# A bias matmul of 64 rows instead of 128, and the gate product issued behind the down product

## The reference

```python
# layer 0: a gated recurrence over the 64 steps, then a mixture of experts (8 experts, the best 2 per token)
gate = sigmoid(h @ Wh.T + z_t @ Wz.T + b);  h = tanh(h * (1 - alpha) + gate * z_t)
gh = einsum('nh,erh->ner', x, W_A)            # routing scores are the norms of gh over r (64)
y  = einsum('nef,ehf->neh', silu(gh @ W_B) * (x @ W_up), W_down)    # F = 512
x  = x + sum over the two chosen experts of y * weight
# layer 1: a tanh recurrence, then a feed-forward block with quantised weights and activations
h  = tanh(x_t @ Wx + b + h @ Wh)
x  = x + bitlinear(gelu(bitlinear(h, w1)), w2)
```

## Time and profile before

| | |
|---|---|
| median of 3 runs | 391.12 us (390.4 to 392.09) |
| the profiled execution's own time | 392.09 us |
| its span, first to last instruction | 390.1 us |
| mean granted TensorE clock | 0.952 of full speed |
| busy share of the span, TensorE | 84% |
| busy share of the span, VectorE | 70% |
| busy share of the span, ScalarE | 60% |
| busy share of the span, GpSimd | 55% |

### The profile page before, as it was taken

One profiled execution on the slowest core, in us unless ns is written; L12 is line 12 of the kernel. 1 busy time (PEld: TensorE's weight loads), 2 busy tenths in 40 slices (PEclk: granted clock), 3 DMA queues, 4 the chain that ended last, 5 costly groups with the idle time before them and its releaser, 6 DMA issues.

```text
span 390.1 us, 11984 instructions
## 1 busy us (share of the span) xinstructions
PE 327.8 (84%) x3816; PEld 231.3 (59%) x3817; DVE 272.2 (70%) x922; ACT 232.7 (60%) x733; POOL 214.0 (55%) x203
## 2 busy tenths in 40 slices
PE   2687777777577789999999999999987999999962
PEld 1444444444353357767777777777675777877841
DVE  5545555567996279587597878544456999999870
ACT  2356656565446446565656565565545878777871
POOL 5659999999804354454444745653115555562220
PEclk9999999998965699999999999999996999999998
DMA  8992185461592133222323332334213122221001
GB/s 209 201 396 103 42 297 188 160 244 64 193 337 75 29 124 89 66 86 68 90 64 91 90 89 73 96 82 79 69 39 97 32 83 69 81 67 41 29 29 40
DMA packets 22536, 42.95 MB, mean 110 GB/s; under 512 B 3986, under 2 KB 14610, under 8 KB 21604
## 3 DMA queue, kind: packets, MB, share of 16 engines
q0 software_dynamic: 6560, 23.17, 19.7%
q1 hardware_dynamic: 15664, 19.31, 15.7%
q10 hardware_dynamic: 276, 0.01, 0.0%
HBM read 28.97 MB, written 13.50 MB: 109 GB/s over the span
## 4 chain that ended last, share of the span: by engine, by line
PE 46%; DVE 14%; ACT 5%; issue 3%; DMA 2%; POOLq 0%; DVEq 0%; POOL 0%; ACTq 0%
PE bank L996 13%; PE bank L972 13%; PE bank L959 4%; PE bank L984 4%; DVE peak L1638 2%; PE bank L950 2%; DVE wrec L1599 2%; DVE h_lo L1669 1%; PE bank L952 1%; PE bank L1094 1%; PE bank L788 1%; PE bank L795 1%; DVE z_lo L1659 1%; PE bank L1111 1%; ACT z_hi L706 1%
## 5 line engine op out<-in xcount | busy, mean ns | idle before, releaser
L497 POOL DMA_INDIRECT xs<-hs_rows,row_of_slot x39 | 37.0, 948 | 72.3 <-PE bank L952 55.7
L788 PE MATMUL bank<-h_hi,wrec_hi 128*128 128x32 f16 x512 | 43.7, 181 | 29.3 <-ACT h_hi L595 27.8
L788 PEld LDWEIGHTS bank<-h_hi,wrec_hi 128*128 128x128 f16 x512 | 34.3, 97 | 56.0 <-ACT h_hi L595 49.6
L972 PE MATMUL bank<-wup_s,xt 128*128 x234 | 64.4, 385 | 0.0
L996 PE MATMUL bank<-wdn_s,wrec 128*128 x468 | 57.8, 273 | 0.3 <-ACT wrec L641 0.3
L996 PEld LDWEIGHTS bank<-wdn_s,wrec 128*128 128x128 f16 x468 | 45.2, 98 | 14.6 <-issue 1.1
L1492 DVE TENSOR_TENSOR wrec<-bank,wrec 128x512 f16<-128x512 f32 x39 | 27.0, 691 | 35.2 <-ACT wrec L641 34.8
L519 POOL DMA_INDIRECT z_lo<-y_rows,slot_i x32 | 31.1, 970 | 27.5 <-issue 26.4
L500 POOL DMA_INDIRECT gs<-gate_rows,row_of_slot x39 | 37.4, 958 | 11.9 <-issue 11.6
L1231 DVE TENSOR_TENSOR_SCAN bank<-bank,terms 128x128 f32<-128x128 f32 x64 | 27.6, 431 | 22.5 <-ACT bank L591 20.6
L788 PE MATMUL bank<-h_hi,wrec_lo 128*128 128x32 f16 x512 | 42.2, 178 | 0.0
(11 more groups left out here) (245 smaller groups left out, 964.1 us busy)
## 6 DMA issues: line engine op xcount, KB each, us to landing
y_rows<-z_lo SPq DMA_DIRECT2D x39, 128.0 KB, 1.8
stage<-wup POOLq DMA_DIRECT2D x2, 2048.0 KB, 10.8
gate_rows<-ga_s SPq DMA_DIRECT2D x16, 256.0 KB, 3.0
stage<-wdn POOLq DMA_DIRECT2D x2, 2048.0 KB, 10.5
stage<-wb SPq DMA_DIRECT2D x2, 1024.0 KB, 14.0
hs_rows<-hs_out SPq DMA_DIRECT2D x16, 128.0 KB, 2.3
stage<-w POOLq DMA_DIRECT2D x2, 1024.0 KB, 7.5
stage<-x_tm POOLq DMA_DIRECT2D x1, 2048.0 KB, 15.0
```

The source lines that it names most:

```text
L497: pool.indirect_dma_start(out=xs[par][:, :], out_offset=None, in_=hs_dram[0:tokens, :], in_offset=bass.IndirectOffsetOnAxis(ap=row_of_slot ...
L788: mm(fm(par)[:, ft, cols], w[:, m, kt, fcols], h_hi[pp][:, kt, pcols], start=False, stop=True, skip_group_check=True)
L972: ins = mm(bank[4 + par][:, :], xt[par][:, b, kt, :], w_slice(wup_s, a, kt, e), start=kt == 0 and n == 0, stop=kt == KT - 1 and n == 2)
```

## The change

It has two parts. `bias_s` has 64 partitions instead of 128, and the bias matmul takes 64 rows of it and of `ones`. And in `expert_tile` on TensorE `gate_product(j + 1)` is issued behind `down(j - 1)` instead of ahead of it. All sums are the same.

```diff
-        bias_s = sb("bias_s", [P, 2, D], F16)
+        bias_s = sb("bias_s", [64, 2, D], F16)
...
-                mm(o, bias_s[:, bias, fcols], ones[:, :], start=ft == 0, stop=False, skip_group_check=True)
+                mm(o, bias_s[:, bias, fcols], ones[0:64, :], start=ft == 0, stop=False, skip_group_check=True)
...
-                if live(j + 1, STILES):
-                    gate_product(j + 1, 1 - par, expert(c + 1))
                 if live(j - 1, STILES):
                     down(j - 1, expert(c - 1))
                 if live(j + 1, STILES):
+                    gate_product(j + 1, 1 - par, expert(c + 1))
                     up(j + 1, 1 - par, 0, expert(c + 1))
```

## The result

The changed kernel takes 402.07 us (median of 6 runs, 401.26 to 403.93), the kernel before 391.5 us in the same measurement (6 runs, 389.65 to 392.09). The ratio is 1.0284, with a 95% interval of 1.0251 to 1.0316: slower by 2.5 to 3.2%, some 10.6 us at the medians.

What follows compares the result with a forecast made beforehand. TensorE was taken as the bound in the expert stage, TensorE and VectorE both near full in the tanh stage. 392.09 + 3.7 (order) + 7.0 (64 rows) = 402.8, or 401.8 us against the median; range 397 to 406.

Steps and rivals of the forecast that it cites:

- The cover of 0.08: Tanh stage, step 2: TensorE time before line 795 starts that hides part of the bias matmul's cost, 0.08 us.
- the two borders: Shape changes before and after each 64-row bias matmul, allowing no overlap with neighbours: 0.31 us for one bias matmul.
- about 0.16 us: Cost of each shape change beside the bias matmul, from a 0.216 us matmul whose neighbour starts after 0.06.
- The count of 13 tiles: Tanh stage: busy tiles from 301.07 to 366.27, each losing 0.54 us on TensorE, 7.0 us in all.
- The third rival: Bias matmul: stationary loads are exposed too, 0.5 us for each bias matmul; 408.5 us in total, chance 0.09.
- Hidden in the gate stage: Gate steps 2 and 3: the bias matmul's 0.31 us lies under 0.39 us of cover, so nothing shows.
- The pause doesn't absorb this: Tanh tile: the wait of up to 0.5 us at line 795 for VectorE doesn't hide the bias matmul's loss.
- the 0.07 us a tile: Expert stage: down released late and running slower loses 0.07 us in each of 37 tiles, 2.6 us.
- the sign that was named: Expert stage: tile longer by 0.07 us, idle time ahead of line 996 put down to line 641, sometimes line 1492.
- The late VectorE: Expert stage: down's second half waits for act_low in five tiles at 0.21 us, 1.1 us in all.
- The free 64-row matmul: The 64-row matmul costs nothing and only the new order shows: 394.8 us, chance 0.22.
- the neutral order: Neither part shows; act_high is done before down's new place and the queue catches up: 391.1 us, chance 0.12.
- The faster case: Down fills TensorE's idle time in the expert stage and 64-row matmuls run beside neighbours: 388.4 us, chance 0.07.

Runs made afterwards that it cites:

- the kernel without register work: New order with 128 rows, down reading expert 0's weights for every tile, against the kernel before the change: ratio 1.0002 (0.9963 to 1.0040).

## Why the prediction came out as it did

401.8 us were predicted with a rise of 10.7; measured were 402.07 and 10.6. Both mechanisms were right, and each has been shown by itself. The two sizes were not: the price of the new order was put at about half of what it is and that of the 64 rows at nearly twice, and the errors cancel. That the total fits so well is luck.

- **The bias matmul, 7.0 us predicted, 3.9 measured (2.6 to 5.2), 3.4 in the stage.** The cover of 0.08 and the two borders stand. The term that was mis-sized is the border, "about 0.16 us": it was worked out as the matmul's recorded 0.216 us less the 0.06 of an ordinary distance. Measured are 0.09. The recorded duration has a modelled end and doesn't say how long a change of shape holds up the next matmul. The count of 13 tiles was too high as well: between the starts of line 772 in step 2 the first two busy tiles take 4.75 and 4.91 us in both traces (from 301.07 to 310.73 before, from 306.58 to 316.24 after) and lose nothing. That is part of why the stage shows less than 13 x 0.31 = 4.0 us. The third rival (the loads exposed too) is refuted with it: line 772's distance to its neighbour leaves no room for 0.1 us more.
- **"Hidden in the gate stage"** was right: 112.5 and 112.4 us, and no cost when only that stage has the 64 rows.
- **"The pause doesn't absorb this"** was right. It was 3.5 us in nine waits, and after, from 320 to 378 us, it is

```profile
PE bank L795 <- DVE h_lo L1668: 3.5, 9, 0.5
```

The reason is in the round of a tile, which goes through both engines. TensorE's matmuls of steps 2, 3 and 0 lead to the subtraction of step 0, and VectorE's queue from there leads to the subtraction that step 2 waits for. Before, the first half had nothing to spare: ScalarE ends the tanh of step 0 at 324.65 and VectorE starts on it at 324.68:

```profile
324.43 0.22 ACT L732 ACTIVATE h<-bank 128x64 f32<-128x64 f32 x1
324.68 0.22 DVE L1669 TENSOR_TENSOR h_lo<-h,h_hi 128x64 f16<-128x64 f32 x1
```

After, VectorE has to wait for it:

```profile
331.05 0.23 DVE L1668 TENSOR_TENSOR h_lo<-h,h_hi 128x64 f16<-128x64 f32 x1 [0.25 <-ACT h L732]
```

So VectorE's idle time absorbed nothing; the delay added to it. Its waits after, 320 to 378 us (us in total, times, longest; before there were 2.0 us in 5 waits from 314 to 372):

```profile
DVE h_lo L1668 <- ACT h L732: 4.0, 13, 0.5
```

- **The moved gate product, 3.7 us predicted, 6.0 measured (3.9 to 7.9), 7.0 in the stage.** The step that failed is the 0.07 us a tile. It was made from the one tile of the trace that has this wait, and that tile happens to be of the cheap kind (the last ALU_OP of line 996 in that trace is at 278.9, a tile earlier). For that kind it was nearly right: 3.90 less 3.81 is 0.09. In every second tile two more register operations come ahead of the first load, down's first matmul starts 0.33 us after the end of `act_high` (243.37 to 243.70) instead of the 0.14 that was taken, and the tile loses 0.29. With both kinds a pair of tiles takes 8.0 us instead of 7.62, 0.19 a tile on average, which was the upper bound of the prediction. And the sign that was named, idle time put down to line 641, didn't come: the profile says "issue".
- **The late VectorE, 1.1 us,** was right in kind and size where it can be seen, in the kernel without register work (five waits, the expert stage 1.3 us longer). In the changed kernel the same wait is 0.4 us in two times: down is slower there, and VectorE gets its time.
- **Rivals.** The free 64-row matmul and the neutral order are each refuted by the kernel with that part alone. The faster case is refuted too: the order alone is 6.0 us slower.

## What to carry to other kernels

A matmul with fewer rows than its neighbours saved nothing here and cost two changes of the array's shape, 0.09 us each; pad such operands with zeros, or, if they must be there, put them side by side and behind work that nobody waits for. Work that stands ahead of a wait covers not only the late operand but also the register work that the queue can do in advance; where a slice is taken with a register, leave that cover or expect a price like the 0.09 and 0.29 us a tile here. And a queue that is "100% busy" can get slower: count its instructions in a window.

## What the hardware showed that I had not expected

Two 64-row matmuls side by side start 0.07 us apart, so between two of one shape 0.01 us is lost, while a single change of shape costs 0.09 us. The price of the same register operations was 6.0 us or nothing, depending on 0.43 us of matmuls ahead of the wait.
